# The last expert layer of a fused transformer kernel: an expert's rows loaded ahead of its weights, results scattered back tile by tile

## The reference, cut to what matters

```
def _moe(x, wg, w1, b1, w2, b2):           # x: 2048 rows of 256, E = 8 experts, FF = 1024
    cap = int(CAP_FACTOR * S) // E          # 256 rows per expert
    gates = jax.nn.softmax(xf @ wg, axis=-1)
    idx = jnp.argmax(gates, axis=-1)
    loc = jnp.sum((jnp.cumsum(mask1, 0) - 1.0) * mask1, -1)
    keep = loc < cap                        # rows over the capacity are dropped
    slot = jnp.where(keep, idx * cap + loc, E * cap)
    disp = zeros((E * cap, D)).at[slot].set(xf, mode='drop')
    h = einsum('ecd,edf->ecf', disp, w1) + b1[:, None, :]
    y = (einsum('ecf,efd->ecd', h, w2) + b2[:, None, :]).reshape(E * cap, D)
    out = where(keep[:, None], gate_val[:, None] * y[slot], 0.0)
y2 = _ln(y1 + _moe(y1, ...), ln2_g, ln2_b)
```

## Time and profile before

| | |
|---|---|
| median of 3 runs | 2447.64 us (2444.84 to 2454.57) |
| the profiled execution, own time | 2451.76 us |
| its span | 2450.0 us, so 1.76 us lie around it |
| mean granted TensorE clock | 0.947 |
| busy: PE, DVE, ACT, POOL | 2099.8, 1269.5, 1010.8, 272.3 us |
| the stage: barrier release after the first norm, first expert product, last result, last norm's first product | 2207.8, 2247.9, 2391.8, 2420.5 us |

### The profile page before, as it was taken

How to read it: one execution, slowest core, us unless ns; L and a number is a source line. 1 busy time by engine, 2 the same in 40 slices (tenths; PEclk the granted TensorE clock), 3 DMA queues, 4 the chain that set the end, 5 groups by cost and what they waited for, 6 DMA issues and landing times. The chain is left out here.

```text
span 2450.0 us, 38336 instructions
## 1 busy us (share of the span) xinstructions
PE 2099.8 (86%) x14693; PEld 1561.0 (64%) x14693; DVE 1269.5 (52%) x2527; ACT 1010.8 (41%) x2844; POOL 272.3 (11%) x357
## 2 busy tenths in 40 slices
PE   6779997899997599689999999969997998874884
PEld 4546765566665489656666666557876776653673
DVE  5447775688885144445545454655435554551003
ACT  3236665677774145223333232433223443331212
POOL 0100000122211534200000000031002000002004
PEclk8989999999999799799999999999999999996986
DMA  3000000121213622230000000010002000021522
GB/s 126 18 1 1 1 2 28 36 56 38 57 33 112 208 61 72 97 130 10 9 9 10 1 9 1 1 31 1 1 1 85 27 10 20 1 86 66 180 95 73
DMA packets 87873, 110.53 MB, mean 45 GB/s; under 512 B 18088, under 2 KB 71344, under 8 KB 86800
## 3 DMA queue, kind: packets, MB, share of 16 engines
q1 hardware_dynamic: 82752, 94.52, 12.6%
q0 software_dynamic: 4944, 13.57, 1.7%
HBM read 77.77 MB, written 22.95 MB: 41 GB/s over the span
## 5 line engine op out<-in xcount | busy, mean ns | idle before, releaser
L920 ACT ACTIVATE ca_prob<-bank,ca_nmax 128x512 f32<-128x512 f32 x256 | 174.0, 690 | 75.6 <-DVE ca_nmax L987 75.6
L920 ACT ACTIVATE na_prob<-bank,na_nmax 128x257 f32<-128x257 f32 x256 | 118.0, 474 | 206.6 <-DVE na_nmax L987 206.6
L987 DVE TENSOR_REDUCE ca_nmax<-bank 128x1 f32<-128x512 f32 x256 | 164.2, 684 | 42.6 <-PE bank L774 42.6
L788 PE MATMUL bank<-cst,ca_prob 128*128 128x128 f32 x1024 | 141.3, 279 | 6.9 <-DVE ca_pT L993 5.2
L788 PEld LDWEIGHTS bank<-cst,ca_prob 128*128 128x128 f32 x1024 | 111.7, 142 | 53.5 <-issue 45.5
L920 ACT ACTIVATE ra_prob<-bank,ra_nmax 128x256 f32<-128x256 f32 x256 | 118.1, 481 | 64.5 <-DVE ra_nmax L987 64.5
L987 DVE TENSOR_REDUCE na_nmax<-bank 128x1 f32<-128x257 f32 x256 | 90.8, 417 | 82.6 <-PE bank L774 82.6
L2142 PE MATMUL bank<-sf_h,sf_W 128*128 128x512 f32 x512 | 120.4, 395 | 0.3 <-DVE sf_h L2214 0.3
L2036 PE MATMUL bank<-na_Wkv,na_cxT 128*128 128x512 f32 x256 | 115.4, 595 | 0.0
L2142 PEld LDWEIGHTS bank<-sf_h,sf_W 128*128 128x128 f32 x512 | 95.8, 187 | 24.3 <-DVE sf_h L2214 1.0
L987 DVE TENSOR_REDUCE ra_nmax<-bank 128x2 f32<-128x512 f32 x128 | 82.1, 684 | 38.5 <-PE bank L774 38.5
(11 more groups left out here) (464 smaller groups left out, 4630.5 us busy)
## 6 DMA issues: line engine op xcount, KB each, us to landing
xl_w<-in_L_ffn_w SPq DMA_DIRECT2D x16, 1024.0 KB, 7.5
rf_sent<-rf_w SPq DMA_DIRECT2D x13, 390.0 KB, 6.3
rf_xin<-rf_sent SPq DMA_DIRECT2D x39, 128.0 KB
dp_cx<-in_ctx_tok SPq DMA_DIRECT2D x4, 1024.0 KB, 14.8
ca_v<-in_ctx_values SPq DMA_DIRECT2D x8, 512.0 KB, 4.5
rf_W<-in_L_ffn_w SPq DMA_DIRECT2D x8, 512.0 KB
rf_rows<-rf_back SPq DMA_DIRECT2D x8, 512.0 KB
na_Wkv<-in_L_xattn_Wkv SPq DMA_DIRECT2D x1, 4096.0 KB, 16.2
```

What stands on the lines that cost most here:

```text
L788: mm = pe.transpose(TB[f % 2][:, j * P:(j + 1) * P], prob[:, n % 2, u, c0:c0 + P], ident)
L920: e = act.activation(prob[:, n % 2, u, hh * keys:(hh + 1) * keys], S[u][:, hh * keys:(hh + 1) * keys], ACT.Exp, bias=nmax[:, n % 2, u, hh: ...
L987: v.tensor_reduce(nmax[:, n % 2, u], S[u][:, 0:W].rearrange("p (h k) -> p h k", h=per), AX.X, ALU.max, negate=True).then_inc(maxed, 1)
```

## The change

A row now carries two more numbers: it is 258 wide instead of 256 in `rows`, `zero` and `sent`. Number 256 holds its token number + 1, number 257 the reciprocal of the softmax sum (the gate value). After the scatter SP loads these pairs for all 2048 slots into `meta` (L2556, 8 bytes for each of 2048 rows), ahead of the rows of expert 0. VectorE makes from them, in four small operations (`find_rows`), the target row of each slot: token + 1, or a spare row for an empty slot. `back` grows to 2T + 1 rows, and four further writes of 512 KB of zeros go into it in the norm phase (L2534), since a dropped token's row has to be zero.

In the expert loop, SP issues the rows of expert e+2 as soon as the transposes of expert e have counted `tn`, and the weights of e+2 after that, when `yc` of e is full; the store to `back` is gone. VectorE multiplies each output tile by its gate column right after the bias. POOL, after each tile, runs a small hold operation and one indirect DMA that scatters the 128 rows to `back`.

At the end SP waits until all 16 scatters have landed and issues four plain loads of 512 KB (L2569). TensorE transposes each pair of tiles straight from `rows`; VectorE only merges.

The diff, cut to its core:

```
-        sent = nc.dram_tensor("xl_sent", (2 * T, D), F32).ap()
-        back = nc.dram_tensor("xl_back", (T, D), F32).ap()
+        sent = nc.dram_tensor("xl_sent", (2 * T, RW), F32).ap()        # RW = D + 2
+        back = nc.dram_tensor("xl_back", (2 * T + 1, D), F32).ap()
 ...                                                     # prefetch, on SP
+                for n in range(T // (4 * P)):
+                    sp.dma_start(back[1 + n * 4 * P:1 + (n + 1) * 4 * P, :].rearrange("(t p) d -> p t d", p=P),
+                                 zero[:, :, 0:D]).then_inc(zs, 16)
 ...                                                     # prepare, on POOL
+                po.tensor_scalar(rows[:, :, D], g.c("token"), 1.0 - T, None, ALU.add).then_inc(numbered, 1)
+                po.tensor_scalar(spare[:], g.c("token"), 1.0, None, ALU.add).then_inc(numbered, 1)
 ...                                                     # sync
                     sp.wait_ge(sent_all, 16 * TT)
+                    sp.dma_start(meta[:], sent[0:T, D:RW].rearrange("(t p) d -> p t d", p=P)).then_inc(meta_in, 16)
                     load_rows(sp, 0)
                     load_rows(sp, 1)
                     for e in range(E):
-                        sp.wait_ge(yc, 2 * e + 2)
                         if e + 2 < E:
+                            sp.wait_ge(tn, e + 1)
+                            load_rows(sp, e + 2)
+                            sp.wait_ge(yc, 2 * e + 2)
                             load_weights(sp, e + 2)
-                            load_rows(sp, e + 2)
-                        sp.dma_start(back[e * CAP:(e + 1) * CAP, :].rearrange("(t p) d -> p t d", p=P), yt[:, e % 2])\
-                          .then_inc(so[e % 2], 16)
+                    for j in range(2):
+                        sp.wait_ge(so[j], 16 * E)
+                    for gi in range(NG):
+                        sp.dma_start(rows[:, 4 * gi:4 * gi + 4, 0:D],
+                                     back[1 + gi * GT:1 + (gi + 1) * GT, :].rearrange("(t p) d -> p t d", p=P))\
+                          .then_inc(got[gi], 16)
 ...                                                     # gpsimd
-                    for j in range(2):
-                        po.wait_ge(so[j], 16 * (E // 2))
-                    hold_pool(g, po).then_inc(held, 1)
-                    for t in range(TT):
-                        po.indirect_dma_start(rows[:, t], None, back, bass.IndirectOffsetOnAxis(ap=fetch[:, t:t + 1], axis=0))\
-                          .then_inc(got[t], 16)
+                    po.wait_ge(addressed, 4)
+                    for n in range(2 * E):
+                        e, t = divmod(n, 2)
+                        po.wait_ge(yc, n + 1)
+                        po.wait_ge(held, n + 1)
+                        hold_pool(g, po).then_inc(held, 1)
+                        po.indirect_dma_start(back, bass.IndirectOffsetOnAxis(ap=dest[:, n:n + 1], axis=0), yt[:, e % 2, t], None)\
+                          .then_inc(so[e % 2], 16)
 ...                                                     # vector, routing
-                    v.reciprocal(inv[:], gate[:]).then_inc(st, 1)
+                    v.reciprocal(rows[:, :, D + 1], gate[:]).then_inc(numbered, 1)
+                    v.wait_ge(numbered, 3)
+                    v.memset(g.hold[:], 0.0).then_inc(st, 1)
 ...
-                    v.tensor_copy(fetch[:], fetchf[:]).then_inc(st, 1)
-                    v.tensor_tensor(gate[:], inv[:], keep[:], ALU.mult).then_inc(st, 1)
 ...                                                     # vector, expert loop
                         if e >= 2:
-                            v.wait_ge(so[e % 2], 16 * (e // 2))
+                            v.wait_ge(so[e % 2], 32 * (e // 2))
                         for t in range(2):
+                            n = 2 * e + t
+                            y = yt[:, e % 2, t]
+                            v.tensor_tensor(y, g.bank[5 + t][:, 0:D], b2[:, e % 2], ALU.add).then_inc(weighted, 1)
+                            v.wait_ge(weighted, n + 1)
+                            v.tensor_scalar(y, y, meta[:, n, 1:2], None, ALU.mult).then_inc(yc, 1)
```

More of the change, by code:

```diff
@@ L2471, in expert_layer @@
             again = sb("again", [P, E, TT])
-            zero = sb("zero", [P, 4, D])
-            rows = sb("rows", [P, TT, D])
+            zero = sb("zero", [P, 4, RW])
+            rows = sb("rows", [P, TT, RW])
+            meta = sb("meta", [P, TT, 2])
+            empty, spare, row = (sb(n, [P, TT]) for n in ("empty", "spare", "row"))
+            dest = sb("dest", [P, TT], U32)
             lg = sb("lg", [P, TT, E])
@@ L2481, in expert_layer @@
             loc = sb("loc", [P, TT, E])
[L2482 to L2483 removed]
+            mx, best, pos, keep, slotf, fetchf, lost, gate = (sb(n, [P, TT]) for n in (
+                "mx", "best", "pos", "keep", "slotf", "fetchf", "lost", "gate"))
             slot = sb("slot", [P, TT], U32)
[L2485 removed]
             w1 = sb("w1", [P, 2, KD, FF])
@@ L2712, in _, with find_rows @@
                     v.tensor_copy(slot[:], slotf[:]).then_inc(st, 1)
-                    v.tensor_copy(fetch[:], fetchf[:]).then_inc(st, 1)
-                    v.tensor_tensor(gate[:], inv[:], keep[:], ALU.mult).then_inc(st, 1)
-                    v.wait_ge(st, 22)
+                    def find_rows():
+                        d = meta[:, :, 0]
+                        v.wait_ge(meta_in, 16)
+                        v.tensor_scalar(empty[:], d, 0.0, None, ALU.is_equal).then_inc(addressed, 1)
+                        v.wait_ge(addressed, 1)
+                        v.tensor_tensor(row[:], empty[:], spare[:], ALU.mult).then_inc(addressed, 1)
+                        v.wait_ge(addressed, 2)
+                        v.tensor_tensor(row[:], row[:], d, ALU.add).then_inc(addressed, 1)
+                        v.wait_ge(addressed, 3)
+                        v.tensor_copy(dest[:], row[:]).then_inc(addressed, 1)
+                        v.wait_ge(addressed, 4)
                     def inputs(e):
@@ L2721, in _ @@
                     inputs(0)
+                    find_rows()
                     for e in range(E):
@@ L2725, in _ @@
                         if e >= 2:
-                            v.wait_ge(so[e % 2], 16 * (e // 2))
+                            v.wait_ge(so[e % 2], 32 * (e // 2))
                         for t in range(2):
[L2728 to L2737, removed]
+                            n = 2 * e + t
+                            v.wait_ge(yp, n + 1)
+                            y = yt[:, e % 2, t]
+                            v.tensor_tensor(y, g.bank[5 + t][:, 0:D], b2[:, e % 2], ALU.add).then_inc(weighted, 1)
+                            v.wait_ge(weighted, n + 1)
+                            v.tensor_scalar(y, y, meta[:, n, 1:2], None, ALU.mult).then_inc(yc, 1)
                     def merge(q):
```

28 lines of the change are left out of this document (14 added, 14 removed).

## The result

The changed kernel takes 2410.03 us (median of 4 runs, 2406.33 to 2410.97), the kernel before 2446.24 us in the runs beside it. The ratio is 0.9847, 95% interval 0.9825 to 0.9869: 36 us or 1.5% faster. The forecast was 2413, with a range of 2404 to 2426.

The account below looks back on a forecast made before the run. TensorE was taken to bound the expert loop, with one hole per expert, and a chain the return. 3.3 + 0.3 + 1.3 - 26.6 - 14.0 = -35.7 us gave 2411.9 or 2416.1; forecast 2413 us, range 2404 to 2426.

Parts of the forecast that it names:

- The hole: Expert loop: TensorE's transposes no longer wait for rows; gain 26.6 us, of which 18.1 waiting, 8.5 clock and restart.
- The rival in which the clock still falls: Expert loop: the lower clock returns although TensorE no longer waits for rows; 8.5 us not gained, 2421; chance 0.12.
- What is late next: Expert loop with shorter periods: rows, weights, VectorE, `so` and POOL all stay covered, at no cost.
- The reason given for the hole: Expert loop: the 256 KB load of rows stood in line behind 2 MB of weights, arriving 7.3 us after its issue.
- The return: After the last result: scatter, four plain loads, transposes and merge take 14.2 us against 28.2; gain 14.0 us.
- The front: Ahead of the expert loop: added zeros cost 3.3 us, the routing memset 0.3, the load of pairs 1.3.
- The first logits product: Start of the stage, a sign that the forecast is right: this product comes at about 2211.
- GpSimd beside VectorE: Expert loop: the gate multiplication could slow POOL's scatters by at most 0.4 us, with the sum unchanged.
- added by hand: Final sum: raised from 2411.9 to 2413 us, since the profiled execution may have had more clock falls than the median run.

Follow-up runs that it names:

- the order alone: Kernel before with only SP's order changed: rows of expert e+2 issued after the transposes of e, ahead of its weights; 2419.65 us, ratio 0.9885.
- the filled hole: Kernel before with 24 transposes of a constant into an unused bank ahead of each wait for rows from expert 2 on; 2440.38 us, ratio 0.9964.
- the variant with the new return alone: Changed kernel with the rows of expert e+2 again issued behind its weights; 2439.52 us, ratio 0.9955.

## Why the prediction was right, step by step

- **The hole** (forecast 26.6, measured 26.9). A period of 14.31 us put together from rows of expert 1 and 7 was measured as 14.25. Both the wait and the low clock behind it went. The rival in which the clock still falls is refuted twice, by the order alone (1.00 throughout) and by the filled hole (1.00 with the loads as late as ever).
- **What is late next: nothing.** Weights, VectorE, `so` and POOL were all costed at zero, and TensorE has no idle time from hidden(1) to hidden(7). That holds only where there is cover: where the hole exists, the 0.4 us of the gate multiplication are paid once per expert, as the variant with the new return alone showed.
- **The reason given for the hole** held too, in its exact form: it was the place behind 2 MB of weights, not the moment of issue. The forecast credited both and did not tell them apart.
- **The return** (forecast 14.0, measured 14.2). Taking the chain from the earlier layer was worth more than adding up parts: 2.94 us was met exactly. 8.1 was 8.6, and the transposes with the last merge took 2.1 instead of 2.8, so two misses, of 0.5 and 0.7 us, cancelled; that the sum was met is luck to this extent.
- **The front** (forecast 3.3 + 0.3 + 1.3, measured 3.4 + 0.5 + 1.35). The queue drains at 343 GB/s by the estimate; 2197.0 to 2203.9 moved 337, and the four writes held SP 5.87 us against 6.1. Both costs were then confirmed by taking them away: 3.4 us at the barrier, 1.1 to 1.5 for the pairs. The first logits product, forecast at about 2211, came at 2203.93; with the 7.25 us that arose ahead of the stage it is 2211.2.
- **GpSimd beside VectorE.** The scatters took 0.98 us each (984 to 987 ns in all sixteen), not 1.37: each multiplication is over before its scatter starts. The Trainium skill's rule (GPSIMD Engine Reference, Key points) was put at 0 on the path, and that fits; no run here shows the contention in this layer.
- **What was missed**, 2.7 us, both in its favour: expert 0 ran 0.9 us faster and the last norm 1.8. Both are matters of the low clock, which the text looked for in the loop alone. The norm's gain belongs to the new return: its first 32 products took 1.94 us in all three profiles with the old return (before, the order alone, the filled hole) and 1.08 in all seven with the new one. That this is because TensorE's work in the return is closer together is the likely reason, but no run isolates it. Expert 0's 0.9 us is mostly luck: hidden(0) to hidden(1) took 17.11 us before and 16.32 in the changed kernel, and 15.9 to 17.0 in the other profiles that have the stop of 30 us ahead of it.

The forecast was 3.0 us above the measured median. 1.4 of these are the kernel before, whose median is 2446.24 beside these runs and was 2447.64 when the forecast was made; 1.1 were added by hand, from 2411.9 to 2413, on the thought that the profiled execution's excess over the median might be clock falls. That thought has no support: this execution lost some 6 us to the stop of ScalarE in another layer, although no profile of a run nearer the median was there to compare. Nor do the times alone bear out the sum. The medians' 36.2 us has an interval of 32 to 43, which can't tell the 35.7 forecast from the 38.4 of the profiles; it is the parts that do.

## What to carry to other kernels

When an engine waits for a small load, look at what stands ahead of it in the same queue before making it earlier: 256 KB behind 2 MB came 3 us late in each period, and swapping the two issues was as good as issuing the small one earlier still. A short stop of TensorE is to be priced at more than its length where the rows show a lower clock behind some of the stops, here 18 us of waiting and 6 to 8 of clock. And DMAs put "beside" a phase still hold its closing barrier for as long as their issue is held by a full queue; if they aren't needed until later, issue them behind it.

## What the runs showed of the hardware

- Stops of 2.9 to 3.7 us of TensorE were followed by the lower clock, 1.2 GHz, in some cases and not in others. In the kernel before it fell not behind the first three (3.04, 2.87 and 2.97 us) but behind the last three (3.10, 2.89 and 3.25 us, with 8.76, 9.60 and 9.51 us for products that take 7.07). In the variant with the new return alone it fell behind four of six, of 3.6 to 3.7 us, and not behind 3.48 and 3.65. With the stops filled or gone it stayed at 2.4 GHz for 85 to 106 us. The length does not decide a single case; what does was not found. The Trainium skill (TensorE: Matmul & The Clock Gate, HAM oscillation) describes a loop whose clock falls at each wait for a load. These runs agree that the falls follow such waits and go with them, but not that each wait brings one.
- A load of 2048 pieces of 8 bytes, 16 KB in all, held up the load behind it by 1.1 us in the pair of profiles that differ in it, 1.5 in the mean of all ten.
- An indirect scatter of 128 rows of 1 KB costs POOL 0.98 us with VectorE idle, and its data had landed, with SP's next issue out, 2.94 us after the end of the operation that made them, in both layers alike.
- ScalarE stood still for 9.3 and 21.8 us in one execution, for a reason that the trace names only as remote, in code where the other nine profiles show nothing of the kind.
